# Three small edits at two stage boundaries of a two-layer transformer kernel on one core

## The chip, the cores and the metric

The kernel is one program on one core of a Trainium2 chip. Its engines are PE (TensorE, matmul and transpose), DVE (VectorE), ACT (ScalarE), POOL (GpSimd) and SP (SyncE, which issues every DMA here). Each runs its own instruction list in order, and they meet only at semaphores. The metric is device microseconds (us) from the first to the last instruction with what lies around it; shorter is better.

## The reference

Two layers, each attention and a feed-forward block on the same layer-normed input, for 2 batches of 1024 rows of 256 numbers. Cut to what matters here:

```python
x = L0_attn_x                                   # (2, 1024, 256)
xn = _layernorm(x)
x = x + L0_attn(xn, Wq, Wk, Wv, Wp, bp) + L0_ffn(xn, W_fc, W_proj)
xn = _layernorm(x)
x = x + L1_attn(xn, wq_a, ..., wo) + L1_ffn(xn, w1, w2, w3)
# L1_attn: latents = xn @ [wq_a; wkv_a].T, rms-normed: q and kv from them, rotary keys, causal softmax
# L1_ffn:  hidden = sigmoid(xn @ w1.T) * (xn @ w2.T), then hidden @ w3.T (w1, w2, w3 ternary)
```

## The kernel before, in words

The program is a chain of stages. Each is a block in which the five engines run their lists; at its end all five meet before the next begins (the waits named L503 and L105 in the profile).

**dense0** computes the first layer's projections and its feed-forward block. The projections go to DRAM (`qk_d`, `v_d`). DVE adds the feed-forward result into `d_x` (L808) and SP stores it to `acc_d` in eight DMAs as its pieces are made (L545). SP then waits for all its stores: the projections' (`stored`, `v_stored`), the eight of `acc_d` (`out`, L550), and for the loads of the first query and key rows into `rows_q` and `rows_k` (`raw_in`).

**attend0** is the first layer's attention in 8 groups of heads. Query and key rows must be reordered in SBUF from `rows_q`, `rows_k` to `a_op_q`, `a_op_k` (from "head part, then token" to "token, then head part"). For group 0, ACT reorders the queries (L1551) while DVE reorders the keys (L1498), each in one instruction of 128x2048; each adds 1 to the semaphore `ordered`. PE's first score and SP's loads for group 1 both wait for `ordered` to reach 2. For later groups POOL reorders both (L1326). POOL's first instructions here are three MEMSETs of `a_v` (L1338), for which SP's loads of values wait.

The stage `ww` adds the attention's output and prepares weights. **d1b0** is the dense part of the second layer for batch 0. It runs several parts one after the other in each engine's list, in the order `loads[0], first, loads[1], norm, rest, f, normed, turn1`:

- `first` (`project1`): PE makes latents; ACT copies them out (L1850) and squares them for the rms norm (L1859).
- `norm` (`layer_norm` with tag `n1`): the layer norm of the *other* batch's rows, batch 1, whose tile `xb[1]` is called `rows_k` in the profile. DVE: statistics (L247, L250), variance plus epsilon (L252); ACT: the root (L261); DVE: the reciprocal (L254) and the eight normed row tiles (L256). PE turns them only in `normed`, after `f`.
- `rest` (`project1`): DVE makes the means of the squares (L1877), ACT the root (L1869), DVE the reciprocal (L1879). POOL makes rotary keys (L1890 to L1893), then, once the reciprocal is there, normed latents (L1896 to L1903).
- `f` (`feed1`): 12 jobs (c, m), 6 for each half c of the rows. PE lifts a job into one of two pairs of PSUM banks in 8 matmuls of 128x512; ACT takes the sigmoid (L2013) and rounds h (L2007); DVE multiplies (L2031, `f1b_h`) and keeps the low part of h (L2024). Lift n waits for product n-2. After lifts 7 and 11 PE drops a half: it multiplies the six high and low tiles by w3 (L1989, L1990).
- `turn1`: PE turns the normed latents and keys that POOL made (L153).

A DVE list is therefore one fixed order: what stands in front of L1877 in it delays L1877.

**d1b1** is the same for batch 1, and the second layer's attention follows to the end of the program.

Of the kernel before, what the change touches and what calls it, by code (L numbers as in the profile page):

```python
# [228 lines left out]

def layer_norm(ph, C, x, came, xn, xt_h, xt_l, banks, before=()):  # L230

    stats = ph.sb("stats", [P, NT, 6])
    mv = ph.sb("mv", [P, NT, 2])
    std = ph.sb("std", [P, NT])
    rstd = ph.sb("rstd", [P, NT])
    S = {n: ph.sem(n) for n in ("ln_step", "var_ready", "std_ready", "rst", "xn_ready", "turned", "high", "low")}
    units = [([xn[:, tt, kt * P:(kt + 1) * P] for tt in range(4 * c, 4 * c + 4)],
              xt_h[:, kt, c * HALF:(c + 1) * HALF], xt_l[:, kt, c * HALF:(c + 1) * HALF])
             for c in range(NCH) for kt in range(KE)]
    ready = [(S["xn_ready"], 4 * c + 4) for c in range(NCH) for kt in range(KE)]  # L240

    def norm(e):
        link = chained(e, S["rst"])
        for tt in range(NT):
            if tt % 2 == 0:
                e.wait_ge(*came[tt // 2])
            e.bn_stats(stats[:, tt, :], x[:, tt, :]).then_inc(S["ln_step"], 1)  # L247
        for tt in range(NT):
            e.wait_ge(S["ln_step"], tt + 1)
            e.bn_aggr(mv[:, tt, :], stats[:, tt, :]).then_inc(S["var_ready"], 1)  # L250
        e.wait_ge(S["var_ready"], NT)
        e.tensor_scalar(std[:, :], mv[:, :, 1], LN_EPS, None, ALU.add).then_inc(S["var_ready"], 1)  # L252
        e.wait_ge(S["std_ready"], 1)
        link(e.reciprocal(rstd[:, :], std[:, :]))  # L254
        for tt in range(NT):
            e.tensor_scalar(xn[:, tt, :], x[:, tt, :], mv[:, tt, 0:1], rstd[:, tt:tt + 1],  # L256
                            ALU.subtract, ALU.mult).then_inc(S["xn_ready"], 1)

    def root(e):
        e.wait_ge(S["var_ready"], NT + 1)  # L260
        e.activation(std[:, :], std[:, :], ACT.Sqrt).then_inc(S["std_ready"], 1)  # L261

    def pe(e):
        for sem, value in before:
            e.wait_ge(sem, value)
        pe_transposes(e, banks, C.ident, units, ready, S["turned"], S["high"], S["low"])

    def act_turn(e):
        act_high(e, banks, units, S["turned"], S["high"])

    def low(e):
        dve_low(e, banks, units, S["high"], S["low"])

    made = Programs(vector=norm, scalar=root), Programs(tensor=pe, scalar=act_turn, vector=low)
    made[1].psum_free = [(S["high"], len(units)), (S["low"], len(units))]
    return made

# [142 lines left out]

def dense0(nc, C, w_p, x_in, weights, bp, qk_d, v_d, acc_d, raw, raw_in):
    Wq, Wk, Wv, Wp, Wfc, Wproj = weights
    with Phase(nc, "d0") as ph:
# [35 lines left out]
            ph.sem(n) for n in ("up", "relu", "squared", "high", "low", "fourth", "joined"))  # L459
        down, sums, mean, root, inverse, biased, added, out = (  # L460
            ph.sem(n) for n in ("down", "sums", "mean", "root", "inverse", "biased", "added", "out"))

# [40 lines left out]
        with nc.Block(no_gpsimd_drain=True) as block:  # L503

            @block.sync
            def _(e):
# [41 lines left out]
                for s in v_stored:  # L548
                    e.wait_ge(s, 16 * B)
                e.wait_ge(out, 16 * B * (NT // 2))  # L550
                for sem in raw_in:
# [668 lines left out]

def attend0(nc, C, qk_d, v_d, ot, m_d, N, sources, rows_in):
    with Phase(nc, "a0") as ph:
# [17 lines left out]
        v_cleared = ph.sem("v_cleared")  # L1240
        ordered = ph.sem("ordered")
        a_scored = ph.sem("a_scored")
# [22 lines left out]
        def bank_b(*user):  # L1265
            return b_banks[AT_B[user] % len(b_banks)]

        def rows(hd):

            return slice(64 * (hd // 2), 64 * (hd // 2) + 64)  # L1270

        with nc.Block(no_gpsimd_drain=True) as block:

            @block.sync
            def _(e):
                def load(g):
                    e.wait_ge(ordered, 2 * g)
                    load_rows(e, qk_d, g, rows_in, landed)

# [26 lines left out]
                for g in range(NG0):  # L1306
# [8 lines left out]
                    if g + 1 < NG0:  # L1315
                        maxima(g + 1, 0)

            @block.gpsimd
            def _(e):
# [15 lines left out]


                for u in range(3):
                    e.memset(v[u][:, :, :, :], 1.0).then_inc(v_cleared, 1)  # L1338
# [16 lines left out]
            def _(e):  # L1355
# [22 lines left out]
                def score_a(g, k):  # L1378
                    hd, i, w = UNITS_A[k]
                    q, kk = ops[g % 3]  # L1380
                    if k == 0:
                        e.wait_ge(ordered, 2 * g + 2)
                    free_a("score", g, k)
                    k0, k1 = w * HALF, min((w + 1) * HALF, (i + 1) * P)
                    e.matmul(bank_a("score", g, k)[:, 0:k1 - k0], q[rows(hd), hd % 2, i * P:(i + 1) * P],  # L1385
                             kk[rows(hd), hd % 2, k0:k1], start=True, stop=True).then_inc(a_scored, 1)
# [138 lines left out]
            def _(e):  # L1525
# [20 lines left out]
                def output(g, c):  # L1546
# [3 lines left out]

                e.activation(ops[0][0][:, :, :].rearrange("p a (t j) -> p (a t) j", j=H0),  # L1551
                             raw[0][:, :, :].rearrange("p j t -> p t j"), ACT.Copy).then_inc(ordered, 1)
                for g in ITERATIONS:
# [389 lines left out]

def feed1(ph, C, W, before, b, xt_h, xt_l, x, x_came, acc_d, spare, down_free=()):
    gate = ph.sb("gate", [P, RING, HALF])
# [72 lines left out]
    def vector(e):  # L2018
# [7 lines left out]
        for n in range(len(jobs)):  # L2026
# [5 lines left out]
            if n >= 1:  # L2032
                rest_h(n - 1)
        rest_h(len(jobs) - 1)
        for tt in range(NT):
# [492 lines left out]
def program(nc, x, Wq, Wk, Wv, Wp, bp, Wfc, Wproj, wq_a, q_ln, wq_b, wkv_a, kv_ln, wkv_b, wo, w1, w2, w3,  # L2528
# [9 lines left out]
    with ExitStack() as ctx:  # L2538
# [13 lines left out]
        with ExitStack() as layer:  # L2552
# [6 lines left out]
            raw_in = [layer.enter_context(nc.semaphore(f"rows_{n}_in")) for n in "qk"]  # L2559
            dense0(nc, C, W.p, x_in, (Wq, Wk, Wv, Wp, Wfc, Wproj), bp, qk_d, v_d, acc_d, rows_in, raw_in)  # L2560
            w_p, W = W.p, Named()
# [6 lines left out]
            with ExitStack() as both:  # L2568
# [6 lines left out]
                ot = wsb("ot0", [P, NG0, T])  # L2575
                attend0(nc, C, qk_d, v_d, ot, m_d, N, (w1, w2, w3), rows_in)
                with Phase(nc, "ww") as ph:
# [8 lines left out]
            with ExitStack() as batch:  # L2586
# [7 lines left out]
                with ExitStack() as dense:  # L2594
# [7 lines left out]
                    with Phase(nc, "d1b0") as ph:  # L2602
                        came = [[ph.sem(f"x{b}{n}_came") for n in range(NT // 2)] for b in range(B)]
                        loads = [load_x(xb[b], source[b], came[b]) for b in (1, 0)]
                        first, rest = project1(ph.part("p1b0"), C, W, cos, sin, kv_ln, *xt[0], *ql[0], keys[0], v[0], "scalar")
                        f = feed1(ph.part("f1b0"), C, W, rest, 0, *xt[0], xb[0], came[0], acc_d,
                                  spare + [tile for pair in q_first for tile in pair])
                        norm, normed = layer_norm(ph.part("n1"), C, xb[1], [(sem, 16) for sem in came[1]],
                                                  xb[1], *xt[1], C.banks[4:8], f.up_free)
                        run(nc, loads[0], first, loads[1], norm, rest, f, normed, turn1(ph.part("t1b0"), C, rest, f))  # L2610
# [41 lines left out]
```

## Time and profile before

| | us |
|---|---|
| three runs | 1294.29, 1298.84, 1300.28 |
| median | 1298.84 |
| the profiled execution, its own time | 1293.62 |
| its span, first to last instruction | 1291.8 |
| d1b0 in the trace | 502.0 to 561.2 |
| from the last matmul of dense0 to the first of attend0 | 154.7 to 162.6 |

All times below are from the profiled execution, in us from the start of its span. A duration in the trace reaches from an instruction's start to its end, and the next one on the same engine can start a little before that end; where a sum needs the pace of a row of instructions, it is the distance between their starts.

### The profile page before, as it was taken

How to read it: one execution, taken by the hardware profiler on the slowest of the kernel's cores; microseconds unless marked ns; L12 is line 12 of the kernel's file. 1: busy time of each engine (PE TensorE's matmuls, PEld its weight loads, DVE VectorE, ACT ScalarE, POOL GpSimd, SP SyncE). 2: the span in 40 equal slices, each digit the busy share in tenths (PEclk: the TensorE clock that was granted, in tenths of full speed). 3: DMA queues.
4: the chain of work that ended last, by engine and by line, in shares of the span. 5: the costliest groups of instructions: out<-in, count | busy, mean ns of one | idle time of the engine just before them, and what ended most of it. 6: DMA issues, size and time to landing. Idle time of an engine off the chain costs nothing.

```text
span 1291.8 us, 22469 instructions
## 1 busy us (share of the span) xinstructions
PE 1178.7 (91%) x7552; PEld 842.2 (65%) x7552; DVE 905.9 (70%) x2340; ACT 744.9 (58%) x1668; POOL 552.4 (43%) x567
## 2 busy tenths in 40 slices
PE   3888698999999888899899999999999999999998
PEld 3776653444443576778677767777767776777688
DVE  7867698899997254566666777666777666777744
ACT  2467326777777235454566666656666656666632
POOL 2336434444341101536445565554565554565310
PEclk9899958999999988899899999999999999999999
DMA  6774154466620474031210111111101310101315
GB/s 195 141 148 77 49 68 59 60 95 91 77 47 2 136 209 140 1 105 65 74 46 17 39 37 45 46 46 30 33 31 45 111 46 17 50 26 53 112 50 179
DMA packets 112467, 93.55 MB, mean 72 GB/s; under 512 B 49697, under 2 KB 102241, under 8 KB 110561
## 3 DMA queue, kind: packets, MB, share of 16 engines
q1 hardware_dynamic: 112352, 92.11, 30.6%
q8 instruction: 61, 1.00, 0.4%
q14 instruction: 54, 0.43, 0.1%
HBM read 53.02 MB, written 30.67 MB: 65 GB/s over the span
## 4 chain that ended last, share of the span: by engine, by line
PE 36%; DVE 12%; issue 3%; ACT 1%; DMA 0%; ACTq 0%; DVEq 0%
PE psum L1049 11%; PE psum L1097 9%; PE psum L194 8%; PE psum L1070 7%; DVE a_part L962 3%; DVE psum L967 3%; DVE a_pt L1000 3%; DVE w L2337 1%; ACT a_p L1014 1%; DVE w_lat L2337 1%; DVE q00l L2337 1%; DVE q01l L2337 1%; DVE a_nm L967 1%; DMA w<-wf_d 0%; DVE ql1l L2218 0%
## 5 line engine op out<-in xcount | busy, mean ns | idle before, releaser
L1031 POOL TENSOR_SCALAR a_p<-a_p,a_rl 128x128 f32<-128x128 f32 (+7 forms) x256 | 218.2, 854 | 300.3 <-DVE a_rl L973 300.3
L1014 ACT ACTIVATE a_p<-psum,a_nm 128x128 f32<-128x128 f32 (+7 forms) x256 | 189.4, 740 | 55.7 <-DVE a_nm L967 54.1
L1532 ACT ACTIVATE a_pt<-psum 128x512 f32<-128x512 f32 (+3 forms) x384 | 167.7, 493 | 71.6 <-PE psum L1395 68.4
L1000 DVE COPY a_pt<-psum 128x512 f32<-128x512 f32 (+1 forms) x192 | 114.5, 596 | 109.0 <-PE psum L1070 108.6
L1070 PE MATMUL psum<-ident,a_p 128*128 128x128 f32 x1152 | 175.4, 279 | 14.2 <-DVE a_pt L1000 14.2
L998 ACT ACTIVATE a_pt<-psum 128x256 f32<-128x256 f32 (+2 forms) x192 | 87.5, 455 | 164.3 <-PE psum L1070 164.2
L1070 PEld LDWEIGHTS psum<-ident,a_p 128*128 128x128 f32 x1152 | 127.2, 140 | 62.3 <-issue 47.8
L1097 PE MATMUL psum<-a_pt,v 128*64 128x256 f32 (+1 forms) x1280 | 159.4, 370 | 1.4 <-ACT rows_k L1111 1.4
L1385 PE MATMUL psum<-a_op_k,a_op_q 64*128 64x512 f32 (+3 forms) x384 | 135.9, 451 | 9.0 <-ACT a_op_q L1551 7.9
L1395 PE MATMUL psum<-a_op_q,a_op_k 64*128 64x512 f32 (+3 forms) x384 | 128.0, 413 | 8.4 <-ACT a_pt L1532 6.9
L1395 PEld LDWEIGHTS psum<-a_op_q,a_op_k 64*128 64x128 f32 x384 | 63.0, 193 | 101.8 <-ACT a_pt L1532 84.8
L1097 PEld LDWEIGHTS psum<-a_pt,v 128*64 128x64 f32 x1280 | 78.4, 136 | 58.0 <-issue 14.7
L962 DVE TENSOR_REDUCE a_part<-psum 128x1 f32<-128x512 f32 x128 | 87.8, 686 | 30.6 <-PE psum L1049 29.5
L1333 POOL TENSOR_SCALAR_AFFINE_SELECT a_pt<-a_pt 128x512 f32<-128x512 f32 x64 | 41.7, 651 | 120.8 <-ACT a_pt L1532 120.7
L1416 PE MATMUL psum<-a_pt,a_v 128*32 128x512 f32 (+3 forms) x768 | 85.7, 519 | 2.5 <-ACT a_oraw L1549 1.2
L967 DVE CUSTOM_DVE_ANT_0 psum<-psum,mask_a 128x128 f32<-128x128 f32 (+3 forms) x128 | 63.5, 496 | 29.0 <-PE psum L1049 28.5
L1385 PEld LDWEIGHTS psum<-a_op_k,a_op_q 64*128 64x128 f32 x384 | 70.1, 205 | 19.9 <-ACT a_op_q L1551 8.1
L1470 DVE TENSOR_REDUCE a_part<-psum 128x1 f32<-128x512 f32 x128 | 82.2, 679 | 0.0
L967 DVE CUSTOM_DVE_ANT_0 psum<-psum,mask_a,a_part 128x128 f32<-128x128 f32 (+3 forms) x128 | 71.4, 558 | 3.9
L1476 DVE CUSTOM_DVE_ANT_0 psum<-psum,mask_a,a_part 128x128 f32<-128x128 f32 (+3 forms) x128 | 66.2, 553 | 8.5 <-PE psum L1385 8.3
L1476 DVE CUSTOM_DVE_ANT_0 psum<-psum,mask_a 128x128 f32<-128x128 f32 (+3 forms) x128 | 59.1, 519 | 11.4 <-PE psum L1385 10.8
L757 POOL TENSOR_TENSOR d_h<-d_r 128x512 f32<-128x512 f32 x32 | 47.2, 1486 | 38.1 <-ACT d_r L699 34.8
(389 smaller groups left out, 2878.6 us busy)
## 6 DMA issues: line engine op xcount, KB each, us to landing
ot_d<-rows_k SPq DMA_DIRECT2D x16, 512.0 KB, 3.0
a_swap<-w_p SPq DMA_DIRECT2D x60, 128.0 KB, 2.3
rows_q<-qk_d SPq DMA_DIRECT2D x48, 128.0 KB, 4.6
rows_k<-qk_d SPq DMA_DIRECT2D x48, 128.0 KB, 7.8
w<-wf_d SPq DMA_DIRECT2D x15, 384.0 KB, 3.4
qk_d<-d_stage_h SPq DMA_DIRECT2D x64, 64.0 KB, 2.1
qk_d<-d_stage_l SPq DMA_DIRECT2D x64, 64.0 KB, 2.1
d_x<-in_L_attn_x_dram SPq DMA_DIRECT2D x8, 256.0 KB, 6.8
```

Of the source, the lines that this page charges most:

```text
L962: e.tensor_reduce(so_far, C.score[t % 2][:, 0:k0], AX.X, ALU.min).then_inc(s.halved, 1)
L967: e.tensor_tensor_reduce(out=tail, in0=tail, in1=C.mask_a[:, HALF - (k1 - k0):HALF], scale=1.0, scalar=so_far, op0=ALU.add, op1=ALU.min, a ...
L1000: e.tensor_copy(dst, src).then_inc(mine, 1)
L1014: e.activation(s.p[:, t % NPB, 0:(i + 1) * P], C.score[t % 2][:, 0:(i + 1) * P], ACT.Exp, scale=-1.0, bias=s.nm[:, k:k + 1], accum_out=s.l ...
L1031: e.tensor_scalar(s.p[:, t % NPB, 0:(i + 1) * P], s.p[:, t % NPB, 0:(i + 1) * P], s.rl[:, k:k + 1], 1.0, ALU.mult, ALU.mult).then_inc(s.no ...
L1049: ins = e.matmul(buf[:, k0:k1], a, bb, start=m == 0, stop=m == len(products) - 1)
L1070: ins = e.transpose(C.turn[par][:, (k - k0) * P:(k - k0 + 1) * P], s.p[:, tt % NPB, k * P:(k + 1) * P], C.ident[:, :])
L1097: ins = e.matmul(out[width * hd:width * (hd + 1), q0:QC], value(2 * n + g, hd, k), s.pt[:, c % 2, hd, k, q0:QC], start=k == 0, stop=k == n ...
L1385: e.matmul(bank_a("score", g, k)[:, 0:k1 - k0], q[rows(hd), hd % 2, i * P:(i + 1) * P], kk[rows(hd), hd % 2, k0:k1], start=True, stop=True ...
L1395: e.matmul(bank_b("score", g, k)[:, off:HALF], kk[rows(hd), hd % 2, j * P:(j + 1) * P], q[rows(hd), hd % 2, c * HALF + off:(c + 1) * HALF] ...
L1476: e.tensor_tensor_reduce(out=bank[:, 0:n], in0=bank[:, 0:n], in1=C.mask_a[:, HALF - n:HALF], scale=1.0, scalar=so_far, op0=ALU.add, op1=AL ...
L1532: e.activation(pt[:, k // G0 % NPT, hd, off:HALF], bank_b("score", g, k)[:, off:HALF], ACT.Exp, scale=-1.0).then_inc(exped, 1)
```

## The change

1. `acc_out` (formerly `out`) becomes a semaphore that outlives dense0. SP no longer waits at the end of dense0 for the eight stores to `acc_d`; it waits for them at the end of its list in attend0. Three semaphores are cleared on POOL behind attend0.
2. The first group's queries are reordered in two halves of 128x1024: ACT does the first, POOL the second as the first instruction of its list in attend0, ahead of the MEMSETs. Its semaphore is `ordered_too`; PE's first score of each group and SP's loads wait for it as well.
3. `layer_norm` is cut into `count` (statistics and variance) and `rows` (reciprocal and normed rows). For the layer norm in d1b0, `norm` does only `count`, and `feed1` calls `rows` for one row tile behind each of its jobs 2 to 9. The first layer norm of this kind, in `ww`, keeps its order.

```diff
-    def norm(e):
-        link = chained(e, S["rst"])
+    def count(e):
         for tt in range(NT):
             if tt % 2 == 0:
                 e.wait_ge(*came[tt // 2])
...
         e.tensor_scalar(std[:, :], mv[:, :, 1], LN_EPS, None, ALU.add).then_inc(S["var_ready"], 1)
-        e.wait_ge(S["std_ready"], 1)
-        link(e.reciprocal(rstd[:, :], std[:, :]))
-        for tt in range(NT):
+
+    def rows(e, first, end):
+        if first == 0:
+            e.wait_ge(S["std_ready"], 1)
+            e.reciprocal(rstd[:, :], std[:, :]).then_inc(S["rst"], 1)
+            e.wait_ge(S["rst"], 1)
+        for tt in range(first, end):
             e.tensor_scalar(xn[:, tt, :], x[:, tt, :], mv[:, tt, 0:1], rstd[:, tt:tt + 1],
                             ALU.subtract, ALU.mult).then_inc(S["xn_ready"], 1)
+
+    def norm(e):
+        count(e)
+        if not rows_apart:
+            rows(e, 0, NT)
...
@@ dense0, SP
                 for s in v_stored:
                     e.wait_ge(s, 16 * B)
-                e.wait_ge(out, 16 * B * (NT // 2))
                 for sem in raw_in:
                     e.wait_ge(sem, ROW_LOADS * 16)
...
@@ attend0
+        def first_queries0(half):
+            t = slice(half * TOK_B // 2, (half + 1) * TOK_B // 2)
+            return (ops[0][0][:, half, :].rearrange("p (t j) -> p t j", j=H0),
+                    raw[0][:, :, t].rearrange("p j t -> p t j"))
...
                 def load(g):
                     e.wait_ge(ordered, 2 * g)
+                    e.wait_ge(ordered_too, 1)
...
+                e.wait_ge(acc_out, 16 * B * (NT // 2))
...
+                e.tensor_scalar(*first_queries0(1), 1.0, 1.0, ALU.mult, ALU.mult).then_inc(ordered_too, 1)
                 for u in range(3):
                     e.memset(v[u][:, :, :, :], 1.0).then_inc(v_cleared, 1)
...
                     if k == 0:
                         e.wait_ge(ordered, 2 * g + 2)
+                        e.wait_ge(ordered_too, 1)
...
-                e.activation(ops[0][0][:, :, :].rearrange("p a (t j) -> p (a t) j", j=H0),
-                             raw[0][:, :, :].rearrange("p j t -> p t j"), ACT.Copy).then_inc(ordered, 1)
+                e.activation(*first_queries0(0), ACT.Copy).then_inc(ordered, 1)
...
@@ feed1, DVE
             if n >= 1:
                 rest_h(n - 1)
+            if row_between and 2 <= n < 2 + NT:
+                row_between(e, n - 2, n - 1)
...
@@ program
+                for sem in (*raw_in, acc_out):
+                    nc.gpsimd.sem_clear(range(sem.num, sem.num + 1))
```

How the order of instructions moves. First DVE's list at the start of d1b0, before (`n_` tiles are the other batch's layer norm, `p1b_ms` the squares' means, `f1b_h` the jobs' products, `k11l` and `q00h` low parts of h):

```order
L247 BN_STATS n_stats<-rows_k 128x6 x8
L250 BN_AGGR n_mv<-n_stats 128x2 x8
L252 TENSOR_SCALAR n_std<-n_mv 128x8
L254 RECIPROCAL n_rstd<-n_std 128x8
L256 TENSOR_SCALAR rows_k<-rows_k,n_mv,n_rstd 128x256 x8
L1877 TENSOR_SCALAR p1b_ms<-p1b_ms 128x8 x2
L1879 RECIPROCAL p1b_ms<-p1b_ms 128x16
L2031 TENSOR_TENSOR f1b_h<-psum,f1b_gate 128x512 x2
L2024 TENSOR_TENSOR k11l<-f1b_h,k10h 128x512
L2031 TENSOR_TENSOR f1b_h<-psum,f1b_gate 128x512
L2024 TENSOR_TENSOR k11l<-f1b_h,k10h 128x512
```

The same place in the list of the changed kernel:

```order
L251 TENSOR_SCALAR n_std<-n_mv 128x8
L1893 TENSOR_SCALAR p1b_ms<-p1b_ms 128x8 x2
L1895 RECIPROCAL p1b_ms<-p1b_ms 128x16
L2047 TENSOR_TENSOR f1b_h<-psum,f1b_gate 128x512 x2
L2040 TENSOR_TENSOR k11l<-f1b_h,k10h 128x512
L2047 TENSOR_TENSOR f1b_h<-psum,f1b_gate 128x512
L2040 TENSOR_TENSOR k11l<-f1b_h,k10h 128x512
L256 RECIPROCAL n_rstd<-n_std 128x8
L259 TENSOR_SCALAR rows_k<-rows_k,n_mv,n_rstd 128x256
L2047 TENSOR_TENSOR f1b_h<-psum,f1b_gate 128x512
L2040 TENSOR_TENSOR q00h<-f1b_h,k10l 128x512
L259 TENSOR_SCALAR rows_k<-rows_k,n_mv,n_rstd 128x256
```

The reciprocal and the eight row tiles left the place ahead of the means and stand singly behind the jobs' products. Second, POOL's list from the end of dense0 into attend0, before (`a_v` are the value tiles, `rows_q` the loaded queries):

```order
L757 TENSOR_TENSOR d_h<-d_r 128x512 x17
L503 UNCONDITIONAL_BRANCH
L84 ISA
L1318 UNCONDITIONAL_BRANCH
L1338 MEMSET a_v 128x1024 x3
L1326 TENSOR_SCALAR a_op_q<-rows_q 128x2048
L1326 TENSOR_SCALAR a_op_k<-rows_k 128x2048
```

And in the changed kernel:

```order
L765 TENSOR_TENSOR d_h<-d_r 128x512 x17
L512 UNCONDITIONAL_BRANCH
L84 ISA
L1333 UNCONDITIONAL_BRANCH
L1352 TENSOR_SCALAR a_op_q<-rows_q 128x1024
L1354 MEMSET a_v 128x1024 x3
L1341 TENSOR_SCALAR a_op_q<-rows_q 128x2048
L1341 TENSOR_SCALAR a_op_k<-rows_k 128x2048
```

One TENSOR_SCALAR over half of the queries now leads POOL's list in attend0. PE's list is the same instructions in the same order in both kernels.

## Rows read from the trace of the kernel before

**Rows 1.** The page: busy time, share of the span and instructions of each engine.

```profile
PE 1178.7 (91%) x7552; PEld 842.2 (65%) x7552; DVE 905.9 (70%) x2340; ACT 744.9 (58%) x1668; POOL 552.4 (43%) x567
```

**Rows 2.** Stretches: PE, PEld, DVE, ACT, POOL busy (count), PE's granted clock, DMA share, GB/s.

```profile
505.00:513.80 8.80, 8.12 (x45) 6.86 (x43) 6.30 (x23) 6.08 (x35) 1.57 (x2) 1.00 0.80 214
513.80:520.00 6.20, 0.01 (x1) 0.00 (x0) 4.26 (x9) 2.58 (x4) 5.43 (x10) 0.76 0.01 3
520.00:523.60 3.60, 3.55 (x8) 2.81 (x9) 1.28 (x2) 0.63 (x1) 2.95 (x8) 0.50 0.00 0
```

**Rows 3.** Timeline, dense0 to attend0: start, us, engine, line, op, [idle before].

```profile
155.64 0.36 SPq L545 DMA_DIRECT2D acc_d<-d_x  x1
158.47 4.08 ACT L1551 ACTIVATE a_op_q<-rows_q 128x2048 fp32r<-128x2048 f32 x1 [7.26 <-PEq L503]
158.50 2.66 DVE L1498 CAST a_op_k<-rows_k 128x2048 fp32r<-128x2048 f32 x1 [2.88 <-PEq L503]
162.61 3.43 PE L1385 MATMUL psum<-a_op_k,a_op_q 64*128 64x128 f32 x10 [7.91 <-ACT a_op_q L1551]
```

**Rows 4.** SP's wait at L550, by its line.

```profile
L550 SPq EVENT_SEMAPHORE  x1: 28/28/28, 157.8 to 157.8; - x1
```

**Rows 5.** Three POOL lines: duration ns min/median/max, first and last start.

```profile
L1338 POOL MEMSET a_v<- x3: 947/948/3225, 158.8 to 162.9; 128x1024 f32 x3
L1326 POOL TENSOR_SCALAR a_op_q<-rows_q x7: 3696/3866/3882, 170.8 to 355.9; 128x2048 fp32r<-128x2048 f32 x7
L1897 POOL TENSOR_SCALAR p1b_qn<-p1b_lat,p1b_ms x16: 317/730/842, 519.3 to 589.4; 128x64 f32<-128x64 f32 x16
```

**Rows 6.** DVE's timeline at the start of d1b0.

```profile
509.40 0.17 DVE L252 TENSOR_SCALAR n_std<-n_mv 128x8 f32<-128x8 f32 x1
511.36 5.06 DVE L256 TENSOR_SCALAR rows_k<-rows_k,n_mv,n_rstd 128x256 f32<-128x256 f32 x8
516.34 0.77 DVE L1877 TENSOR_SCALAR p1b_ms<-p1b_ms 128x8 f32<-128x8 f32 x2
519.30 1.29 DVE L2031 TENSOR_TENSOR f1b_h<-psum,f1b_gate 128x512 f32<-128x512 f32 x2 [1.66 <-ACT f1b_gate L2013]
```

**Rows 7.** ACT's timeline there.

```profile
510.77 0.21 ACT L1859 ACTIVATION_READ_ACCUMULATOR p1b_qn<-p1b_lat 128x1 f32 x1
517.38 1.28 ACT L2013 ACT_TABLE_LOAD   x1
```

**Rows 8.** PE's timeline: lift 2, drop 0, lift 8, turns of latents.

```profile
520.05 0.79 PE L194 MATMUL psum<-ql1h,w 128*128 128x512 f32 x1 [6.24 <-DVE f1b_h L2031]
...
532.82 0.28 PE L1989 MATMUL psum<-w,k10h 128*128 128x256 f32 x1
...
538.57 0.40 PE L194 MATMUL psum<-ql1h,w 128*128 128x512 f32 x1
...
554.08 1.91 PE L153 MATMUL psum<-ident,p1b_qn 128*128 128x128 f32 x16
```

**Rows 9.** The row tiles of both layer norms, by line L256.

```profile
L256 DVE TENSOR_SCALAR ww_xn<-o0b_x,n_mv,n_rstd x8: 406/406/411, 455.2 to 457.5; 128x256 f32<-128x256 f32 x8
L256 DVE TENSOR_SCALAR rows_k<-rows_k,n_mv,n_rstd x8: 406/858/898, 511.4 to 515.5; 128x256 f32<-128x256 f32 x8
```

**Rows 10.** DVE's timeline in the jobs, between lifts and near the end.

```profile
526.39 0.69 DVE L2031 TENSOR_TENSOR f1b_h<-psum,f1b_gate 128x512 f32<-128x512 f32 x1 [0.61 <-ACT f1b_gate L2013]
527.00 0.71 DVE L2024 TENSOR_TENSOR q00h<-f1b_h,k10l 128x512 fp32r<-128x512 f32 x1
532.44 1.40 DVE L2024 TENSOR_TENSOR q00l<-f1b_h,k11h 128x512 fp32r<-128x512 f32 x1
```

**Rows 11.** POOL's timeline in the jobs.

```profile
512.15 0.86 POOL L1890 TENSOR_TENSOR p1b_rot<-p1b_lat,p1b_ct 128x256 f32<-128x256 f32 x1 [9.05 <-DMA p1b_lnw<-in_L_attn_kv_a_ln_w_dram]
...
531.99 1.31 POOL L1901 TENSOR_TENSOR v<-p1b_vs,p1b_lnw 128x512 f32<-128x512 f32 x1
...
535.08 1.29 POOL L1903 TENSOR_TENSOR p1b_kk<-p1b_vs,p1b_lnw 128x512 f32<-128x512 f32 x1
```

More of the change, by code:

```diff
@@ L224, in _, with layer_norm @@
                 e.tensor_scalar(C.mask_a[:, HALF - P:HALF], maskf[:, :], -1.0, None, ALU.mult)
-def layer_norm(ph, C, x, came, xn, xt_h, xt_l, banks, before=()):
+def layer_norm(ph, C, x, came, xn, xt_h, xt_l, banks, before=(), rows_apart=False):
     stats = ph.sb("stats", [P, NT, 6])
@@ L275, in layer_norm @@
     made[1].psum_free = [(S["high"], len(units)), (S["low"], len(units))]
+    made[0].rows = rows
     return made
@@ L418, with dense0 @@
 LOWS_P = [sum(kind == "qk" for kind, _, _ in JOBS_P[:n]) for n in range(N_P + 1)]
-def dense0(nc, C, w_p, x_in, weights, bp, qk_d, v_d, acc_d, raw, raw_in):
+def dense0(nc, C, w_p, x_in, weights, bp, qk_d, v_d, acc_d, raw, raw_in, out):
     Wq, Wk, Wv, Wp, Wfc, Wproj = weights
@@ L459, in dense0 @@
             ph.sem(n) for n in ("up", "relu", "squared", "high", "low", "fourth", "joined"))
-        down, sums, mean, root, inverse, biased, added, out = (
-            ph.sem(n) for n in ("down", "sums", "mean", "root", "inverse", "biased", "added", "out"))
+        down, sums, mean, root, inverse, biased, added = (
+            ph.sem(n) for n in ("down", "sums", "mean", "root", "inverse", "biased", "added"))
         def tile(w, kt, mt):
@@ L1218, in load_rows, with attend0 @@
                             qk_d[part_, m, 2 * g + blk]).then_inc(landed[m], 16)
-def attend0(nc, C, qk_d, v_d, ot, m_d, N, sources, rows_in):
+def attend0(nc, C, qk_d, v_d, ot, m_d, N, sources, rows_in, acc_out):
     with Phase(nc, "a0") as ph:
@@ L1240, in attend0 @@
         v_cleared = ph.sem("v_cleared")
-        ordered = ph.sem("ordered")
+        ordered, ordered_too = ph.sem("ordered"), ph.sem("ordered_too")
         a_scored = ph.sem("a_scored")
@@ L1938, in turn1, with feed1 @@
     return Programs(tensor=tensor, scalar=scalar, vector=vector)
-def feed1(ph, C, W, before, b, xt_h, xt_l, x, x_came, acc_d, spare, down_free=()):
+def feed1(ph, C, W, before, b, xt_h, xt_l, x, x_came, acc_d, spare, down_free=(), row_between=None):
     gate = ph.sb("gate", [P, RING, HALF])
@@ L2559, in program @@
             raw_in = [layer.enter_context(nc.semaphore(f"rows_{n}_in")) for n in "qk"]
-            dense0(nc, C, W.p, x_in, (Wq, Wk, Wv, Wp, Wfc, Wproj), bp, qk_d, v_d, acc_d, rows_in, raw_in)
+            acc_out = layer.enter_context(nc.semaphore("acc_out"))
+            dense0(nc, C, W.p, x_in, (Wq, Wk, Wv, Wp, Wfc, Wproj), bp, qk_d, v_d, acc_d, rows_in, raw_in, acc_out)
             w_p, W = W.p, Named()
@@ L2575, in program @@
                 ot = wsb("ot0", [P, NG0, T])
-                attend0(nc, C, qk_d, v_d, ot, m_d, N, (w1, w2, w3), rows_in)
+                attend0(nc, C, qk_d, v_d, ot, m_d, N, (w1, w2, w3), rows_in, acc_out)
+                for sem in (*raw_in, acc_out):
+                    nc.gpsimd.sem_clear(range(sem.num, sem.num + 1))
                 with Phase(nc, "ww") as ph:
@@ L2604, in program @@
                         loads = [load_x(xb[b], source[b], came[b]) for b in (1, 0)]
+                        up_free = []
                         first, rest = project1(ph.part("p1b0"), C, W, cos, sin, kv_ln, *xt[0], *ql[0], keys[0], v[0], "scalar")
+                        norm, normed = layer_norm(ph.part("n1"), C, xb[1], [(sem, 16) for sem in came[1]],
+                                                  xb[1], *xt[1], C.banks[4:8], up_free, rows_apart=True)
                         f = feed1(ph.part("f1b0"), C, W, rest, 0, *xt[0], xb[0], came[0], acc_d,
-                                  spare + [tile for pair in q_first for tile in pair])
-                        norm, normed = layer_norm(ph.part("n1"), C, xb[1], [(sem, 16) for sem in came[1]],
-                                                  xb[1], *xt[1], C.banks[4:8], f.up_free)
+                                  spare + [tile for pair in q_first for tile in pair], row_between=norm.rows)
+                        up_free += f.up_free
                         run(nc, loads[0], first, loads[1], norm, rest, f, normed, turn1(ph.part("t1b0"), C, rest, f))
```

## The prediction, on record before the changed kernel was run

> **What bounds the kernel now.** I read four views in this order: the page's busy shares, the busy time by stretch, the timeline of each engine around the two places that the change touches, and single lines with their spread of durations. The page gives PE 91% of the span, DVE 70% and POOL 43% [rows 1]. PE sets the pace, so only what makes PE wait is worth anything, and the change leaves PE's list as it is. It can gain in two gaps of PE.
>
> The first gap is the meeting between dense0 and attend0. SP issues the last store to `acc_d` at 155.64 for 0.36 [rows 3] and is let past it at 157.8 [rows 4]; the engines start at 158.47 [rows 3]. ACT then reorders the queries in 4.08, and PE's first score starts at 162.61, after 7.91 of idling that the trace puts down to ACT.
>
> The second gap is in d1b0. Between 513.80 and 520.00 PE is busy for 0.01; its clock was granted in full (1.00) before, and behind the gap it is 0.50 of full speed, the lower of its two levels, for 3.6 [rows 2]. PE's lift 2 waits 6.24 for product 0 [rows 8]. Follow it back: product 0 starts at 519.30 behind the sigmoid [rows 6], that behind a table load at 517.38 [rows 7], that behind the root of the means, which DVE makes at 516.34 [rows 6]. The squares that the means need had ended on ACT at 510.98 [rows 7]. Between lies a single group: the eight row tiles of the other batch, 511.36 to 516.42, which nobody needs before the turns at about 552.
>
> **The change part by part.**
>
> *The stores awaited later.* SP passes on after its last issue, at 156.00, instead of at 157.83. The six waits ahead of L550 were done inside that wait and are now behind the last issue. I allow them 0.2 in all, an estimate from the 28 ns of such a wait [rows 4]. Start of attend0: 1.6 earlier. DVE's last work ends at about 155.6, so nobody else is later. The moved wait comes at the end of attend0's list on SP, hundreds of us after the stores' landing. The three clears stand on an idle POOL: nothing.
>
> *Half the queries on POOL.* ACT's half is 4.08 / 2 = 2.04. POOL's instruction of the same kind takes 3.70 for 2048 at its fastest [rows 5], so 1024 take about 1.9. Side by side with DVE's 2.66 all would be over after 2.7, and PE would start 4.14 - 2.69 = 1.4 earlier. But one row speaks against it. POOL's three MEMSETs are of one size; two took 0.947 and the first 3.225 [rows 5]. It started at 158.82, inside DVE's CAST of the keys (158.50 to 161.16 [rows 3]), and 3.225 - 0.947 = 2.28 later than 158.82 is 161.10, the end of the CAST. So POOL did nothing while that CAST ran. POOL's first instruction starts 0.35 behind ACT's, DVE's 0.03 behind. POOL's half then waits for the CAST and ends at 161.10 + 1.9 = 163.0 on the clock of before, where ACT's whole piece ended at 162.55. Were POOL first, the CAST would wait for it, with the same sum (1.9 + 2.66). I take +0.5 for PE and for SP's loads of group 1, which wait for the same two semaphores. Net at this boundary: 1.6 - 0.5 = 1.1 gained.
>
> The Trainium skill says this too (SBUF — State Buffer, section "SBUF: two separate sides"): DVE and GpSimd share one pair of ports as an exclusive lock, and whichever comes second is fully blocked if DVE's instruction is in a two-port mode. The MEMSET's row agrees. By the lock the boundary gives 1.1, without it 3.0.
>
> The MEMSETs behind POOL's half end some 7.5 after the start (4.6 + 3 x 0.95), SP's twelve loads ahead of the value loads end near 10. They hide it.
>
> *The rows between the jobs, first part.* The means can start when the squares are in, 511.05 instead of 516.34. They took 0.77, since POOL's products ran beside them (from 512.15 [rows 11]); alone they should take about 0.3. The rest of the chain to PE, 520.05 - 517.11 = 2.94, is unchanged and waits for no lift: product 0 at 513.6, lift 2 at 514.3, against 520.05. That is 5.75. PE then idles 0.5 instead of 6.2, and its clock should stay at the upper level. Lift 2 at the lower clock ran from 520.05 to 523.62, where eight such matmuls at the upper take 1.81 (lifts 4 to 7 run with that pace until 532.82 [rows 8]); a ninth was part slow. That is 1.9 more. From 514.3 six lifts of 1.81 end at 525.2, against 532.82: 7.6 gained, if DVE keeps up.
>
> *Second part: does DVE keep up?* A job costs DVE 0.61 for the product and about 0.6 for the low part [rows 10], and it idled 0.5 to 0.6 before the next [rows 10]. A row tile paces at 0.33 alone (406 ns long), but 858 ns is its median length beside POOL [rows 9]. 0.61 + 0.61 + 0.33 = 1.55 fits in 1.81. A product may be some 0.3 late before PE feels it: product 3 ended at 527.08 [rows 10], and lift 5 began at 527.38. So each job bears 0.26 + 0.3 of blocking. The low part (two inputs in SBUF) and the row tile can both be blocked by POOL: the low part at 532.44 took 1.40 beside POOL's 1.31 [rows 10, 11]. Up to lift 7, POOL runs products of 0.73 and then pieces of 0.32 to 0.42. Stepping through the jobs, I find products 2 to 5 late by 0 to 0.5, lift 7 late by 0.1. In drop 0 (5.75 of PE alone, 532.82 to 538.57 [rows 8]) DVE catches up. Lifts 8 to 11 then run from 531.1, and here POOL's three instructions of 1.3 [rows 11] come at 533 to 538, since the rows also hold POOL up by 1 to 2. Two low parts and one row tile are blocked by them. Product 9 is 1.35 late, lift 11 waits 0.9, and drop 1, which needs the low part of job 9, another 0.5 or so. I take 1.5. The bounds are 0 (POOL elsewhere) and 4 (half the jobs as the second rival has them). Gain in d1b0: 7.6 - 1.5 = 6.1.
>
> POOL's chain ended at 536.37 [rows 11] and will end near 538. PE needs it for the turns of the latents at 554.08 [rows 8] less 6.1, that is 548. Hidden by 10.
>
> *Sum.* 1.1 + 6.1 = 7.2. On the profiled execution, 1293.62 - 7.2 = 1286.4. That execution was 5.2 below the median of the runs shown, and below their lowest. On the median it is **1298.84 - 7.2 = 1291.6**, a gain of 0.55%. What a measurement of this kernel can tell from no change is 0.5%, 6.5. The forecast sits just past that.
>
> **The rivals.**
>
> *No lock* (0.15). POOL's half runs beside the CAST, and the POOL pieces fall between DVE's. For it: POOL's products at 512 to 516 were not slowed by the row tiles beyond the first (0.86). Against it: the 3.225 MEMSET. It gives 1.6 + 1.4 + 7.6 = 10.6: 1288.2.
>
> *DVE becomes the bound in d1b0* (0.25). If every job pays for two blockings, 0.61 + 1.40 + 0.86 = 2.87 against 1.81, 1.06 a job, 8.5 over eight jobs, all of the 7.6 and more. If half of them do, 4.2. With the boundary's 1.1 the time lies between 1294.3 and 1298.6. For it: the medians in [rows 9]. Against it: from 519 on POOL's pieces are short, and drop 0 gives DVE 5.75 to catch up.
>
> *Slower: POOL becomes late* (0.05). Each of its 35 instructions in this stage can be held up by DVE; the 128x64 ones took 0.842 where 0.317 is their shortest [rows 5], 0.52 each. If all pay this and eight pay 0.31 more for a row, POOL ends 20.7 later, at 557.1. PE would wait for it from 548.0, 9.1, more than the 7.2: 1300.7. It decides from a slip of about 18 on. Against it: only some ten of them met a DVE instruction before.
>
> *It does nothing at the first boundary*, where another wait ends last: if the start moves by 0.2 only, the loss of 0.5 stays and the whole gives 5.8, 1293.0. That is within the forecast's 0.55, whose own range is 1289.5 to 1294.3.
>
> **How the numbers follow.** Forecast 0.55, no lock 0.15, DVE bound 0.25, slower 0.05. The range runs from the no-lock case less 1.2 to within the DVE-bound case, with the runs' own spread (1294.29 to 1300.28) in mind: 1287.0 to 1296.5. Faster by over 0.5%: all of no lock, and 0.40 of the forecast's 0.55, since a gain of 7.2 read with an error of a few tenths of a per cent can fall short: 0.55. Within 0.5%: the rest of the forecast and the DVE-bound case, 0.40. Slower: 0.05.
>
> **What the profile of the changed kernel would show.** The start of attend0 about 1.6 earlier, near 156.9. POOL's first instruction there near 4.2 long, not 1.9, ending at about the time when DVE's CAST has been over for 1.9; PE's first score at about 161.5, waiting for POOL. In d1b0, counted from its start: the means within 0.3 of the last square, PE's idle time before lift 2 about 0.5, no stretch at clock 0.50 behind it, row tiles of 0.4 to 1.6, a wait of about 1 before lift 11. The first thing that would make me wrong is POOL's phase in jobs 7 to 10, then an effect of the shifted start on later stages, which I take as moving unchanged.

## The result, and the profile after

The changed kernel takes 1292.35 in the median of 20 runs, the kernel before 1301.28 in 20. The ratio is **0.993, with a 95% interval of 0.9913 to 0.9947**: 9.1 faster, between 6.9 and 11.3. The forecast was a gain of 7.2, and a time of 1291.6 from the earlier median of 1298.84. A second measurement gave 0.9912 (0.9885 to 0.9939).

The page of the changed kernel, its span and the busy times that answer to [rows 1]:

```profile
span 1287.5 us, 22482 instructions
PE 1180.2 (92%) x7552; PEld 840.8 (65%) x7552; DVE 905.6 (70%) x2340; ACT 745.3 (58%) x1668; POOL 551.4 (43%) x568
```

The two profiled executions differ by 4.3 only (spans of 1291.8 and 1287.5), less than half of the 9.1. Spans of single executions mislead here. Over 20 executions of the changed kernel the time follows PE's mean granted clock: 1285.23 at 0.965, 1289.24 (the profiled one) at 0.961, 1298.11 at 0.953, correlation -0.94. That spread of 13 lies within one and the same kernel, so no edit makes it. From the start of attend0 to that of d1b0 the profiled execution of before took 343.4, and all eleven later ones, changed or not, 348.1 to 354.1. The granted clock of two stretches in it, first before, then after:

```profile
200.00:240.00 40.00, 36.42 (x251) 16.32 (x249) 35.22 (x105) 28.51 (x66) 18.82 (x13) 0.91 0.55 66
360.00:400.00 40.00, 37.79 (x280) 16.67 (x278) 37.51 (x114) 29.78 (x73) 12.17 (x14) 1.00 0.11 25
```

```profile
200.00:240.00 40.00, 36.64 (x248) 16.20 (x246) 33.97 (x100) 27.81 (x64) 18.46 (x14) 0.87 0.55 62
360.00:400.00 40.00, 37.75 (x270) 16.49 (x266) 35.87 (x110) 29.11 (x70) 11.55 (x14) 0.96 0.11 26
```

It was lower in both after the change, in work that the change does not touch. The edits are not the reason, as far as the runs tell: the kernel with only the third edit took 354.1 there and the one with only the first two 352.0, and these two share no edit. The kernel before was profiled only once. So everything below is read as a distance between two events of one stage, not as a span.

**The boundary of dense0 and attend0**, timeline of the changed kernel (DVE's last adds, then the three engines that reorder, then PE); answers to [rows 3] and [rows 5]:

```profile
153.58 0.88 DVE L816 SCALAR_TENSOR_TENSOR d_x<-psum,d_rms,d_x 128x256 f32<-128x256 f32 x2 [0.81 <-PE psum L603]
155.66 3.10 ACT L1568 ACTIVATE a_op_q<-rows_q 128x1024 fp32r<-128x1024 f32 x1 [5.60 <-PEq L512]
155.68 3.04 DVE L1515 CAST a_op_k<-rows_k 128x2048 fp32r<-128x2048 f32 x1 [1.22 <-PEq L512]
156.06 4.40 POOL L1352 TENSOR_SCALAR a_op_q<-rows_q 128x1024 fp32r<-128x1024 f32 x1 [13.48 <-POOLq L512]
160.41 2.73 POOL L1354 MEMSET a_v<- 128x1024 f32 x3
160.60 2.89 PE L1402 MATMUL psum<-a_op_k,a_op_q 64*128 64x128 f32 x9 [7.06 <-POOL a_op_q L1352]
```

DVE's idle time ahead of its CAST is 1.22, against 2.88 in [rows 3]: the start moved 1.66 forward. POOL's half took 4.40 instead of 1.9, and ended 1.74 after the CAST. PE waited for it, 4.94 from start to first score, against 4.14.

**d1b0.** All times of this table count from the stage's first load (at 501.89 before, 503.76 after).

| | before | after | gained so far |
|---|---|---|---|
| lift 2 | 18.16 | 12.34 | 5.82 |
| drop 0 | 30.93 | 23.68 | 7.25 |
| lift 8 | 36.68 | 29.44 | 7.24 |
| drop 1 | 44.41 | 38.14 | 6.27 |
| first load of d1b1 | 59.32 | 53.23 | 6.09 |

The clock, the number behind POOL's, in stretches of the changed kernel, for [rows 2]:

```profile
515.70:519.00 3.30, 2.91 (x14) 2.41 (x14) 1.77 (x4) 1.87 (x4) 3.07 (x4) 1.00 0.02 6
519.00:527.50 8.50, 8.47 (x38) 6.69 (x37) 7.93 (x15) 4.83 (x9) 7.30 (x14) 1.00 0.00 0
533.20:541.00 7.80, 7.21 (x32) 5.35 (x31) 6.88 (x9) 4.04 (x7) 4.62 (x5) 1.00 0.00 0
```

It stays at the upper level. PE's idle time before lift 2 fell from 6.24 to 0.39. DVE's timeline in jobs 3 and 4 and behind drop 0, for [rows 10]:

```profile
521.73 0.68 DVE L2040 TENSOR_TENSOR q00h<-f1b_h,k10l 128x512 fp32r<-128x512 f32 x1
522.33 0.40 DVE L259 TENSOR_SCALAR rows_k<-rows_k,n_mv,n_rstd 128x256 f32<-128x256 f32 x1
522.66 0.68 DVE L2047 TENSOR_TENSOR f1b_h<-psum,f1b_gate 128x512 f32<-128x512 f32 x1
...
534.12 1.53 DVE L2040 TENSOR_TENSOR k11l<-f1b_h,k10h 128x512 fp32r<-128x512 f32 x1 [5.15 <-ACT k10h L2023]
535.57 1.38 DVE L259 TENSOR_SCALAR rows_k<-rows_k,n_mv,n_rstd 128x256 f32<-128x256 f32 x1
536.87 0.68 DVE L2047 TENSOR_TENSOR f1b_h<-psum,f1b_gate 128x512 f32<-128x512 f32 x1
```

And POOL and PE beside it, for [rows 11]:

```profile
533.79 1.31 POOL L1917 TENSOR_TENSOR v<-p1b_vs,p1b_lnw 128x512 f32<-128x512 f32 x1
535.18 1.62 POOL L1918 TENSOR_TENSOR p1b_kk<-p1b_vs,p1b_lnw 128x512 f32<-128x512 f32 x1
536.88 1.27 POOL L1919 TENSOR_TENSOR p1b_kk<-p1b_vs,p1b_lnw 128x512 f32<-128x512 f32 x1
```

```profile
537.61 0.50 PE L194 MATMUL psum<-ql1h,w 128*128 128x512 f32 x1 [0.59 <-DVE f1b_h L2047]
```

Among POOL's short pieces a row tile costs 0.40. Beside the pieces of 1.3 the low part takes 1.53 and the row tile 1.38, so product 8 starts 1.0 later than its gate (ACT's sigmoid, ready at 535.84) allows, and lift 10 waits. That is the wait of 0.59 before PE's row.

### The profile page after: what moved, and what is told of

The parts are those of the page before. It is cut to its first block, busy times and chain, and to the rows that moved or that the text cites. A ratio compares the mean times of both kernels' runs of the same rounds, so it can differ in the third digit from the quotient of the medians.

```text
span 1287.5 us, 22482 instructions
## 1 busy us (share of the span) xinstructions
PE 1180.2 (92%) x7552; PEld 840.8 (65%) x7552; DVE 905.6 (70%) x2340; ACT 745.3 (58%) x1668; POOL 551.4 (43%) x568
## 4 chain that ended last, share of the span: by engine, by line
PE 36%; DVE 12%; issue 4%; ACT 1%; DMA 0%; ACTq 0%; DVEq 0%
PE psum L1057 11%; PE psum L1105 9%; PE psum L194 8%; PE psum L1078 7%; DVE a_part L970 3%; DVE psum L975 3%; DVE a_pt L1008 3%; DVE w L2355 1%; ACT a_p L1022 1%; DVE w_lat L2355 1%; DVE q00l L2355 1%; DVE q01l L2355 1%; DVE a_nm L975 1%; DMA w<-wf_d 0%; DVE ql1l L2236 0%
## 5 line engine op out<-in xcount | busy, mean ns | idle before, releaser
L765 POOL TENSOR_TENSOR d_h<-d_r 128x512 f32<-128x512 f32 x32 | 43.2, 1361 | 41.0 <-ACT d_r L707 37.8
```

## The experiments

Theory: the row tiles carry the change. At the first boundary the early start gives 1.7, and POOL's half gives a part back, since POOL is locked out while DVE's CAST runs. In d1b0 about 1 is lost where row tiles and POOL's three long instructions meet. Rivals: the first boundary carries the gain; POOL's half helps; the loss in d1b0 comes from the row tiles alone or from POOL alone.

**Only the row tiles** (the wait for the stores in dense0 and ACT's full reordering restored):

```diff
+                e.wait_ge(out, 16 * B * (NT // 2))
...
-                e.activation(*first_queries0(0), ACT.Copy).then_inc(ordered, 1)
+                e.activation(ops[0][0][:, :, :].rearrange("p a (t j) -> p (a t) j", j=H0),
+                             raw[0][:, :, :].rearrange("p j t -> p t j"), ACT.Copy).then_inc(ordered, 1)
```

> Only the third edit (the row tiles between the jobs); the stores are awaited in dense0 and ACT reorders all queries, as before. If the row tiles carry the change, d1b0 (from its first load to that of d1b1) takes 53.2 as in the changed kernel, against 59.3 before, and the whole is 6.1 faster than before, ratio 0.995. If the gain came from the first boundary, d1b0 stays near 59 and the ratio is 1.000. From the start of attend0 to PE's first score: 4.1, as before.

Measured: ratio 0.9945 (0.9918 to 0.9972), d1b0 in 53.49. The row tiles carry most of the change: the distances within d1b0 show it, while the intervals of the ratios overlap. Its own span was 1297.3, at a clock of 0.951: one more case where the span of one execution says the wrong thing.

**Without POOL's half:**

```diff
-                e.tensor_scalar(*first_queries0(1), 1.0, 1.0, ALU.mult, ALU.mult).then_inc(ordered_too, 1)
...
-                e.activation(*first_queries0(0), ACT.Copy).then_inc(ordered, 1)
+                e.activation(ops[0][0][:, :, :].rearrange("p a (t j) -> p (a t) j", j=H0),
+                             raw[0][:, :, :].rearrange("p j t -> p t j"), ACT.Copy).then_inc(ordered, 1)
```

> The changed kernel without its second edit: ACT reorders all queries alone. If POOL is locked out while DVE's CAST runs, PE's first score comes 4.1 after the start of attend0, against 4.94 in the changed kernel, so this kernel is about 0.8 faster than the changed one. If the split helped, the first score comes later here than in the changed kernel. DVE's CAST takes 2.66 again rather than 3.04. Ratio to before about 0.994.

Measured: ratio 0.9925 (0.9894 to 0.9957), not to be told from the changed kernel's. The first score came at 4.85, not 4.1: ACT took 4.79 and the CAST 3.00 with nothing of POOL's reordering. So the CAST's 3.04 in the changed kernel need not have been POOL's doing, and the expected 0.8 was a comparison of two single executions. Over the kernels that start these instructions together the first score comes at 4.14, 4.28, 4.49 and 4.85 with ACT alone, and at 4.62, 4.66, 4.72 and 4.94 with POOL's half, means of 4.44 and 4.74. POOL's half costs about 0.3, with ranges that overlap. That it would give 1.4 is ruled out. Its d1b0 took 52.32. That goes with POOL's chain, which began 9.40 after the stage's first load and not 10.15; its long instructions lay 0.9 earlier, and PE hardly waited before lift 10. There the low part behind drop 0 ran in 0.71 and only the row tile was blocked (1.38), so product 8 started 2.86 behind lift 8, against 3.67 in the changed kernel and 2.68 where nothing is blocked. How much is lost in d1b0 therefore goes with where POOL's chain happens to lie: the seven profiled executions with row tiles between the jobs and POOL's long instructions in their old place took 52.3 to 53.5.

**Without the row tiles' move:**

```diff
-                                                  xb[1], *xt[1], C.banks[4:8], up_free, rows_apart=True)
+                                                  xb[1], *xt[1], C.banks[4:8], up_free)
...
-                                  spare + [tile for pair in q_first for tile in pair], row_between=norm.rows)
+                                  spare + [tile for pair in q_first for tile in pair])
```

> The changed kernel without its third edit: the row tiles stand ahead of the means again. First and second edit give together 1.6 - 0.8 = 0.8, so the ratio to before is 0.9994, no change that can be measured; d1b0 takes 59.3 again, with a wait of about 6.2 before lift 2 and the lower clock behind it. If the first boundary carried the gain, the ratio would be 0.994.

Measured: ratio 0.9984 (0.9963 to 1.0005), no change that can be told, as expected. d1b0 took 60.98. The wait before lift 2 was 6.74 this time, and the clock stayed down longer. Stretches from there, for [rows 2]:

```profile
526.70:530.30 3.60, 3.55 (x8) 2.81 (x9) 1.29 (x2) 0.63 (x1) 2.95 (x8) 0.50 0.00 0
530.30:534.00 3.70, 3.70 (x12) 2.90 (x11) 1.29 (x2) 1.52 (x3) 3.05 (x8) 0.64 0.00 0
```

A second lift ran mostly at the lower level. From lift 2 to drop 0, six lifts that take 11.01 to 11.04 in the six kernels where nothing holds them up, it took 12.77 in the profiled execution of before and 13.94 in this one: the gap costs 1.7 by the clock there and 2.9 here.

**All row tiles in drop 0**, without POOL's half:

```diff
+            if row_between and n == HT1 + 1:
+                row_between(e, 0, NT)
             if n >= 1:
                 rest_h(n - 1)
-            if row_between and 2 <= n < 2 + NT:
-                row_between(e, n - 2, n - 1)
```

> No split, and all eight row tiles in DVE's list behind product 7, where DVE waits about 5.2 for drop 0. If the row tiles in jobs 8 and 9 helped to make products 9 and 10 late, the waits before lifts 10 and 11 shrink from 0.76 to at most 0.3, the 0.33 before lift 5 goes, and d1b0 takes 52.2 to 52.6 instead of 53.2. If POOL's three instructions of 1.3 alone did it, only the 0.33 before lift 5 goes: about 52.9. If POOL is held up by eight row tiles in a row, its chain ends up to 3 later, at no cost. Ratio to before about 0.993.

Measured: ratio 0.9904 (0.9874 to 0.9934), d1b0 in 51.75, below what was expected: both waits, before lift 5 and lift 10, are gone. The rest from lift 8 to drop 1 is 7.78, against 7.73 before the change, though POOL's three instructions lie at the same place (30.17 to 35.0 from the first load). The ratio is not to be told from those of the changed kernel, and part of what d1b0 gains is given back behind it: d1b1 takes 56.64 here and 56.02 in the changed kernel, so the two stages together take 108.4 against 109.3.

**POOL's long instructions held back** until DVE has kept the last low part (`hold` is feed1's semaphore `low` at 12), else the changed kernel:

```diff
+        for sem, value in hold:
+            e.wait_ge(sem, value)
         weight = lnw[:, :].unsqueeze(1).to_broadcast([P, NT, KL])
         link(e.tensor_tensor(v[:, :, :], vs[:, :, :], weight, ALU.mult))
```

> The changed kernel with POOL's last three instructions of d1b0 (128x512 each) held back until DVE has kept the last low part. If these three made products 9 and 10 late, the wait of 0.76 before lift 10 is gone, drop 1 starts 8.7 - 1.2 = 7.5 after lift 8, and the row tiles in jobs 8 and 9 take 0.41. If the row tiles themselves did it, nothing changes. POOL then ends 3.9 after DVE's last low part, ahead of the turns of the latents, so d1b0 takes about 52.0 rather than 53.2.

DVE's timeline of this kernel behind drop 0:

```profile
535.30 0.69 DVE L2044 TENSOR_TENSOR k11l<-f1b_h,k10h 128x512 fp32r<-128x512 f32 x1 [5.15 <-ACT k10h L2027]
535.91 0.41 DVE L259 TENSOR_SCALAR rows_k<-rows_k,n_mv,n_rstd 128x256 f32<-128x256 f32 x1
537.05 0.69 DVE L2051 TENSOR_TENSOR f1b_h<-psum,f1b_gate 128x512 f32<-128x512 f32 x1 [0.73 <-ACT f1b_gate L2033]
```

0.69 and 0.41 where the changed kernel has 1.53 and 1.38, DVE waits for its gate again, d1b0 takes 51.77 (expected 52.0), and the wait before lift 10 is gone. With POOL's instructions and no row tiles the loss is absent, and with row tiles and no POOL too. It takes both, and in an unfavourable phase, as the kernel without POOL's half shows. Each of these is one execution.

The kernel with POOL held back and the next three ran once each: 1289.93, 1289.35, 1290.88 and 1294.37 in this order, with 1299.28 for the kernel before beside them. With 13 between executions of one kernel, these times say nothing about one against another, so only distances within a stage are read.

**POOL first**: DVE's CAST waits for POOL's half.

```diff
+                e.wait_ge(ordered_too, 1)
                 e.tensor_copy(ops[0][1][:, :, :].rearrange("p a (t j) -> p (a t) j", j=H0),
```

> The changed kernel with DVE's CAST of the keys held back until POOL has reordered its half of the queries. If the two never run side by side, the order is indifferent: POOL takes 1.9 from 0.35 on, the CAST 2.7 behind it, first score 4.9 to 5.0 after the start of attend0 (4.94 and 4.62 in the two kernels with POOL's half). If they could share, this order costs a full 1.9 more than the changed kernel, 6.8. POOL's instruction takes 1.9 here, not 4.4.

The three engines in this kernel, then PE:

```profile
156.12 1.95 ACT L1569 ACTIVATE a_op_q<-rows_q 128x1024 fp32r<-128x1024 f32 x1 [5.60 <-PEq L512]
158.48 3.85 DVE L1516 CAST a_op_k<-rows_k 128x2048 fp32r<-128x2048 f32 x1 [3.56 <-POOL a_op_q L1352]
156.52 1.93 POOL L1352 TENSOR_SCALAR a_op_q<-rows_q 128x1024 fp32r<-128x1024 f32 x1 [13.51 <-POOLq L512]
158.39 4.84 POOL L1354 MEMSET a_v<- 128x1024 f32 x3
162.39 3.44 PE L1402 MATMUL psum<-a_op_k,a_op_q 64*128 64x128 f32 x10 [8.38 <-DVE a_op_k L1516]
```

Measured: the first score came at 6.27, neither 4.9 nor 6.8. POOL's half takes 1.93 alone, as expected; the 4.40 of the changed kernel was waiting. What the expectation missed is that POOL's first MEMSET starts at 158.39, ahead of the CAST. The three MEMSETs by their line (shortest, median, longest in ns, first and last start):

```profile
L1354 POOL MEMSET a_v<- x3: 948/949/3056, 158.4 to 160.2; 128x1024 f32 x3
```

Two of them run in 0.95 each, from 158.39 to about 160.2, and the CAST, which starts at 158.48, takes 3.85, 1.44 more than the 2.41 that it takes alone (in the experiment with the CAST behind ACT's reordering, below). The third, started at 160.2, takes 3.06 and ends 0.9 after the CAST. So the CAST was held up by the first MEMSETs, for longer than one of them lasts, and the last MEMSET by the CAST. The order is not indifferent: the CAST in second place waits also behind MEMSETs that nobody is in a hurry for. In d1b0 of this kernel (53.10) PE's wait, of 0.96, came before lift 11.

**DVE takes the second half of the queries**, behind its keys:

```diff
-                e.tensor_scalar(*first_queries0(1), 1.0, 1.0, ALU.mult, ALU.mult).then_inc(ordered_too, 1)
...
+                e.tensor_copy(*first_queries0(1)).then_inc(ordered_too, 1)
```

> The changed kernel with the second half of the queries reordered by DVE, behind its keys, and nothing of it on POOL. DVE then needs 2.7 + 1.35 = 4.05, or up to 4.6 at the slower pace that its CAST showed in some runs; first score 4.1 to 4.7, against 4.94. POOL's MEMSETs are locked out until DVE is done, so the first takes about 4.6.

DVE's and POOL's timeline:

```profile
157.00 2.68 DVE L1514 CAST a_op_k<-rows_k 128x2048 fp32r<-128x2048 f32 x1 [1.22 <-PEq L512]
159.62 1.00 DVE L1516 CAST a_op_q<-rows_q 128x1024 fp32r<-128x1024 f32 x1
157.33 5.96 POOL L1353 MEMSET a_v<- 128x1024 f32 x3 [13.41 <-POOLq L512]
```

Measured: first score at 3.78, better than expected. DVE does half of the queries in 1.00, half of POOL's 1.93, and without a wait. The first MEMSET waited for both CASTs and took 4.18.

**The CAST behind ACT's reordering**, to measure both alone (no split):

```diff
+                e.wait_ge(ordered, 1)
                 e.tensor_copy(ops[0][1][:, :, :].rearrange("p a (t j) -> p (a t) j", j=H0),
```

> The kernel without the split, with DVE's CAST held back until ACT has reordered all queries; it measures both alone. If the two hold each other up, ACT takes about 2.0 for 2048 at one element a cycle of 1.2 GHz and a fixed part, rather than 4.1 to 4.8, and the CAST 2.2 to 2.7. If ACT is simply slow on this pattern, it takes 4.1 alone too, and the first score comes at 6.9.

```profile
156.71 3.71 ACT L1566 ACTIVATE a_op_q<-rows_q 128x2048 fp32r<-128x2048 f32 x1 [5.60 <-PEq L512]
160.45 2.41 DVE L1513 CAST a_op_k<-rows_k 128x2048 fp32r<-128x2048 f32 x1 [4.93 <-ACT a_op_q L1566]
157.06 2.74 POOL L1352 MEMSET a_v<- 128x1024 f32 x3 [13.42 <-POOLq L512]
```

ACT is slow on this pattern by itself, 3.71, far from 2.0. But both are faster apart than side by side. The first score came at 6.21, not 6.9. With no CAST beside them the three MEMSETs take 2.74.

**The version that the runs point to**: stores awaited later, row tiles in drop 0, three quarters of the queries on ACT and a quarter on DVE. It ran with the changed kernel on the same chip.

```diff
-                e.activation(*first_queries0(0), ACT.Copy).then_inc(ordered, 1)
+                e.activation(*quarter_queries0(2), ACT.Copy)
+                e.activation(*first_queries0(0), ACT.Copy).then_inc(ordered, 1)
...
+                e.tensor_copy(*quarter_queries0(3)).then_inc(ordered_too, 1)
```

> The version that the runs point to: stores awaited later, all eight row tiles behind product 7, nothing of the reordering on POOL, and of the queries ACT reorders three quarters (a quarter and a half) and DVE the last quarter behind its keys. By the pieces seen (ACT 2.4 for a half beside the CAST, so about 3.4 to 3.6 for three quarters in two instructions; DVE 2.7 + 0.55) the first score comes 3.4 to 3.8 after the start, against 4.94 in the changed kernel. d1b0 takes 51.8, against 53.2. Both together 2.7 faster than the changed kernel, 11.8 faster than before by its measured 0.993, ratio to before about 0.991. If ACT's two instructions cost more than the pieces say, the first score comes at 4.1 or later and the ratio is that of the kernel without split, 0.992.

> The changed kernel once more, on the same chip as the version with a quarter on DVE, so that the two can be compared: ratio to before 0.993 by its measurement, 0.9944 by the sum of the prediction.

```profile
155.76 1.54 ACT L1575 ACTIVATE a_op_q<-rows_q 128x512 fp32r<-128x512 f32 x1 [5.60 <-PEq L512]
157.12 2.02 ACT L1576 ACTIVATE a_op_q<-rows_q 128x1024 fp32r<-128x1024 f32 x1
158.42 0.59 DVE L1523 CAST a_op_q<-rows_q 128x512 fp32r<-128x512 f32 x1
159.19 3.44 PE L1408 MATMUL psum<-a_op_k,a_op_q 64*128 64x128 f32 x10 [5.54 <-ACT a_op_q L1576]
```

Measured: first score at 3.43, d1b0 in 51.76. Both are where they were expected. The ratio was 0.9925 (0.9896 to 0.9954), that of the changed kernel beside it 0.9912 (0.9885 to 0.9939). By stage distances the version gains 1.3 at the boundary against its neighbour (3.43 and 4.72) and 1.6 in d1b0 (51.76 and 53.40), and loses 0.7 in d1b1 (56.69 and 56.03). The sum of 2.3 is below what the runs can tell, and they do not show it as faster; the 2.7 that was expected over the changed kernel is not confirmed.

## Why the prediction was right

The gain forecast lies within the interval of the measured one: 7.2 forecast, 6.9 to 11.3 measured. That the time itself, 1291.6, came within 0.8 of 1292.35 is luck: the median of before rose by 2.4 with more runs (1298.84 to 1301.28), and the measured gain is larger than the forecast by about as much. Stage by stage:

- *The stores awaited later*: 1.6 forecast, 1.66 measured. ACT's idle time before attend0 is 5.59 or 5.60 in each kernel that awaits them later, and 7.26 and 7.27 in the two that do not.
- *Half the queries on POOL*: a loss of 0.5 forecast, from the one MEMSET that had been 2.28 too long. In the profiled pair it was 0.8, over four kernels of each kind about 0.3. The mechanism is shown (1.93 alone, 4.07 to 4.40 beside the CAST). The size was off in both directions because ACT's and DVE's own durations vary, which no row of before could tell.
- *The means ahead of the row tiles*: lift 2 5.75 earlier forecast, 5.82 measured, and the clock stays at the upper level. The term of 1.9 for the clock is 1.7 when the same six lifts are compared (12.77 against 11.03), in the one execution that it was read from; another one paid 2.9.
- *Does DVE keep up*: 1.5 lost forecast, 1.5 measured (5.82 + 1.74 for the clock - 6.09): 0.31 before drop 0 (it starts 11.34 behind lift 2, where six lifts held up by nothing take 11.03), 0.97 from lift 8 to drop 1 beyond what these took before, the rest behind. I had 0.1 for the first. For the second, two low parts and one row tile blocked were forecast, and these were blocked (1.53, 1.38 and, behind product 8, 1.23), but the place was one job off. I had POOL's chain 1 to 2 later, and lift 11 waiting for product 9. POOL ended where it had ended, 34.4 and 34.5 from the first load, so its long instructions met the first low part and row tile behind drop 0, and lift 10 waited for product 8. That the sum came out so close is in part luck: the same work lost between 0.6 and 1.7 in d1b0 over seven executions (52.3 to 53.5, where 51.8 is the time without the loss), by where POOL's chain lay.
- *Later stages unchanged*: d1b1 took 56.02 instead of 56.64, 0.6 that I had not counted.

The parts that are shown add up to 1.66 - 0.80 + 6.09 + 0.62 = 7.6. The ratio says 9.1. The difference of 1.5 is inside the interval, and the runs do not say whether it is real; a gap before lift 2 that costs more by the clock than 1.7 in most executions would be one reason, and was not tested over many.

*No lock* gave 1288.2 and is out: POOL's half did wait, and row tiles were blocked. *DVE as the bound* was right in its mechanism only where POOL's long instructions lay, for two jobs of eight. *POOL late* did not happen. *Nothing at the first boundary* is out by the 1.66.

## What to carry to other kernels

Look for work that nobody needs soon in front of work on which the matrix engine waits, in the list of one engine. Moving it paid twice here, since the clock did not drop behind the gap. Where there is a choice, put it into a stretch in which that engine idles anyway (the drop), rather than evenly between jobs: that was worth about 1.5 in d1b0 and 0.9 over d1b0 and d1b1 together, too little to show in the whole time. Handing half of a reordering to POOL while DVE copied from SBUF to SBUF added the two durations instead of overlapping them; ACT ran beside DVE, each of them somewhat slower, and POOL did not.

## What was not expected of the hardware

ACT and DVE slow each other in this reordering. ACT takes 1.95 for the half without the CAST (POOL's half ran beside it) and 2.34, 2.40, 2.44, 2.52 or 3.10 beside the CAST, which takes 2.67, 2.68, 2.71, 2.76 and 3.04 in the same kernels; for the whole 3.71 without the CAST and 4.08, 4.23, 4.44 or 4.79, with CASTs of 2.66, 2.70, 2.83 and 3.00; the CAST alone takes 2.41. The two grow together in either list. "Alone" is one execution each. The Trainium skill (SBUF — State Buffer, section "SBUF: two separate sides") says that ACT never waits on anyone on the engine side of SBUF. These runs speak against that for two strided reads side by side. What sets how much they pay in an execution stays open. POOL's reordering took 1.93 for a half in the one kernel where it ran without the CAST, and 3.65 to 3.74 for the next group's queries in all kernels.

d1b1 takes 56.0 in five of the kernels whose d1b0 had a wait before lift 10 or 11 (52.9 to 53.5), 56.4 in the sixth, and 56.6 to 56.8 in the six without it, the kernel before among them. So a wait there costs less in the end than d1b0 by itself shows, by about 0.6 in five of six. Why is open.
